# Routing five of eight batches inside the first attention instead of after it

## The reference, cut to what matters

```python
x = x + (o @ wo + bo)                         # end of the first attention (z in the kernel)
hn2 = layernorm(x, ln2_g, ln2_b).reshape(-1, 128)
logits = hn2 @ gate_w + gate_b                # 8 experts
idx = argmax(logits, axis=-1)                 # the first of equal ones
mid = relu(hn2 @ w1[e] + b1[e])               # 128 -> 512, for each expert e
y = mid @ w2[e] + b2[e]                       # 512 -> 128
moe = y[idx, token]                           # each token takes its own expert's row
```

## Time and profile before

| | us |
|---|---|
| median of three executions | 1964.28 |
| the profiled execution | 1971.45 |
| its span in the trace | 1969.7 |
| attention_l0, first reduce to last add | 339.5 to 711.1 |
| moe, first instruction to the first tile's transpose | 712.3 to 772.4 |
| moe, the loop over 40 tiles | 772.4 to about 885 |

### The profile page before, as it was taken

The page is one execution under the profiler, slowest core; times in us unless marked ns, Lnnn a source line. Parts: engine busy times, 40 slices in busy tenths (PEclk is TensorE's granted clock), DMA queues, the critical chain, the costliest instruction groups (busy, mean ns, idle before and its releaser), DMA issues. The chain is left out here.

```text
span 1969.7 us, 48105 instructions
## 1 busy us (share of the span) xinstructions
PE 1733.4 (88%) x18438; PEld 740.2 (38%) x18438; DVE 1569.2 (80%) x2889; ACT 1310.2 (67%) x2776; POOL 1120.2 (57%) x740
## 2 busy tenths in 40 slices
PE   6528856999999974986998999999999999999997
PEld 3327732233333353663442333333333333333334
DVE  7953467999999833547878999999999999999973
ACT  4502234789989932225884777888888878888885
POOL 8813542000100035331133988999999999989995
PEclk9869877799999975998997999999999999999998
DMA  2230036111111052117995323323223232232311
GB/s 49 33 55 3 1 100 241 40 50 40 49 40 50 23 177 71 50 48 256 367 405 164 88 73 81 86 68 88 73 81 87 66 88 75 78 83 70 87 29 43
DMA packets 194487, 180.14 MB, mean 91 GB/s; under 512 B 58740, under 2 KB 155124, under 8 KB 194052
## 3 DMA queue, kind: packets, MB, share of 16 engines
q1 hardware_dynamic: 185860, 170.01, 29.3%
q0 software_dynamic: 2944, 7.10, 1.1%
q10 hardware_dynamic: 5504, 0.73, 0.2%
HBM read 101.16 MB, written 75.26 MB: 90 GB/s over the span
## 5 line engine op out<-in xcount | busy, mean ns | idle before, releaser
L1038 ACT ACTIVATE probs_l<-exp_l 128x512 f32<-128x512 f32 x1024 | 575.6, 595 | 177.4 <-PE exp_l L1077 171.6
L976 DVE TENSOR_REDUCE maxima_l<-max_l 128x1 f32<-128x512 f32 x1024 | 640.1, 683 | 32.9 <-PE max_l L1122 32.9
L952 POOL TENSOR_TENSOR part_sums_l<-probs_l 128x1024 f32<-128x1024 f32 x256 | 604.1, 2360 | 91.7 <-ACT probs_l L1038 78.8
L1077 PE MATMUL exp_l<-q_stack_l,k_stack_l 100*128 100x512 f16 x1024 | 392.0, 384 | 3.3 <-ACT probs_l L1038 2.9
L1122 PE MATMUL max_l<-k_stack_l,q_stack_l 96*128 96x512 f16 x1024 | 386.8, 388 | 4.6 <-DVE pv_bank_l L968 3.8
L1361 DVE TENSOR_REDUCE maxima_l<-max_l 128x1 f32<-128x512 f32 x512 | 317.0, 682 | 16.7 <-PE max_l L1465 16.5
L1415 ACT ACTIVATE probs_l<-exp_l 128x512 f32<-128x512 f32 x512 | 279.3, 600 | 42.5 <-PE exp_l L1478 37.1
L1093 PE MATMUL pv_bank_l<-probs_l,v_ring_l 128*32 128x512 f32 x2048 | 273.9, 607 | 0.5 <-ACT probs_l L1038 0.5
L1077 PEld LDWEIGHTS exp_l<-q_stack_l,k_stack_l 100*128 100x128 f16 x1024 | 98.4, 97 | 395.0 <-ACT probs_l L1038 363.8
L1297 POOL TENSOR_SCALAR rstd_l<-squares_l 128x4 f32<-128x4 f32 x7 | 1.6, 235 | 344.6 <-ACT junk_l L1400 344.6
L958 POOL TENSOR_TENSOR part_sums_l<-part_sums_l 128x512 f32<-128x512 f32 x128 | 163.1, 1274 | 10.0
(11 more groups left out here) (303 smaller groups left out, 2454.9 us busy)
## 6 DMA issues: line engine op xcount, KB each, us to landing
scratch_qk_l<-parts_g SPq DMA_DIRECT2D x128, 256.0 KB, 9.4
q_stack_l<-scratch_qk_l SPq DMA_DIRECT2D x192, 128.0 KB
k_stack_l<-scratch_qk_l SPq DMA_DIRECT2D x192, 128.0 KB
scratch_v_l<-v_g SPq DMA_DIRECT2D x16, 1024.0 KB
v_ring_l<-scratch_v_l SPq DMA_DIRECT2D x64, 256.0 KB, 3.3
scratch_stack_l<-parts_c SPq DMA_DIRECT2D x16, 384.0 KB, 3.5
q_stack_l<-scratch_stack_l SPq DMA_DIRECT2D x64, 96.0 KB, 2.2
k_stack_l<-scratch_stack_l SPq DMA_DIRECT2D x64, 96.0 KB, 2.3
```

The lines of the kernel that those rows point to most:

```text
L952: pool.tensor_tensor(part_sums[:, i, h, :, :], probs[:, i, h, 0:2, :], probs[:, i, h, 2:4, :], ALU.add).then_inc(pair_sum.sem, 1)
L976: dve.reduce_max(maxima[:, s % 2, at % NT, at // NT:at // NT + 1], max_bank(n, at)[:, :], AX).then_inc(max_taken.sem, 1)
L1038: act.activation(probs[:, i, at // NT, at % NT, :], exp_ps[at % 2][:, :], ACT.Exp, scale=a.scale).then_inc(prob_tile.sem, 1)
L1077: pe.matmul(exp_ps[at % 2][:, :], ks[0:SHIFT_ROW + HG, slot, h, k * P:(k + 1) * P], qs[0:SHIFT_ROW + HG, slot, h, :], start=True, stop=Tru ...
```

## The change

Batches 0 to 4 are routed wholly inside `attention_l0`, one turn each, in turns 3 to 7. Batch b is handled in turn b + 3:

- PE, s = 1, p = 7: four transposes of its normalised rows into `misc`; ScalarE, s = 2, first position: the affine step `hT` from `misc`.
- PE, s = 2, p = 7: four narrow matmuls for its logits, and the two rank matmuls of batch b - 1, both into `misc`; ScalarE, s = 3, first position: one copy of both to SBUF (`scores`).
- GpSimd adds the gate's bias, VectorE takes at s = 3, p = 6 the maximum and the equality with it (two instructions with a wait between them), GpSimd makes the rest of the choice with products of "none so far" (`choose`), and then, one batch behind, the places (`destine`) and the four scatters.
- GpSimd now also waits at the end of the stage for all its 20 scatters.

`moe` keeps only batches 5, 6 and 7: 12 scatters in place of 32.

```diff
-ROWS_BESIDE = B - 1
+ROWS_BESIDE, ROUTED_BESIDE = B - 1, 5
+L0_ROWST_STEP, L0_LOGITS_STEP, L0_BEST_AT = 1, 2, 6
...
+            def choose(b):
+                at = slice(b * NT, (b + 1) * NT)
+                pool.wait_ge(scores_sb.sem, scores_sb.made(b, 0))
+                pool.tensor_tensor(logits[:, :, :], scores[:, 0, :, :], r.gate_b[:, :].unsqueeze(1).broadcast_to([P, NT, E_]),
+                                   ALU.add).then_inc(logits_taken.sem, 1)
...
+                pool.wait_ge(is_best_ready.sem, is_best_ready.made(b, 0))
+                did(pool.tensor_tensor(none_so_far[:, 0, :, :], ones_e[:, :, :], is_best[:, :, :], ALU.subtract))
+                settle()
+                for n, step in enumerate((1, 2, 4)):
+                    old, new = none_so_far[:, n % 2, :, :], none_so_far[:, (n + 1) % 2, :, :]
+                    did(pool.tensor_copy(new[:, :, 0:step], old[:, :, 0:step]))
+                    did(pool.tensor_tensor(new[:, :, step:E_], old[:, :, step:E_], old[:, :, 0:E_ - step], ALU.mult))
+                    settle()
...
+            def destine(b):
...
+                for width in (4, 2, 1):
+                    did(pool.tensor_tensor(place[:, :, 0:width], place[:, :, 0:width], place[:, :, width:2 * width], ALU.add))
+                    settle()
+                did(pool.tensor_copy(r.dest[:, at], place[:, :, 0]))
...
+                for k in range(b * NT, (b + 1) * NT):
+                    pool.indirect_dma_start(out=sorted_rows[:, :], out_offset=bass.IndirectOffsetOnAxis(r.dest[:, k:k + 1], 0),
+                                            in_=r.rows[:, k, :], in_offset=None).then_inc(scattered, 16)
...
+                if 0 <= b - 1 < ROUTED_BESIDE:
+                    choose(b - 1)
+                if 0 <= b - 2 < ROUTED_BESIDE:
+                    destine(b - 2)
+            pool.wait_ge(rows_ready.sem, rows_ready.made(ROWS_BESIDE - 1, 0))
+            pool.wait_ge(scattered, 16 * ROUTED_BESIDE * NT)
...
+                    if p == L0_BEST_AT and s == L0_LOGITS_STEP + 1 and 0 <= turn - 3 < ROUTED_BESIDE:
+
+                        dve.wait_ge(logits_taken.sem, logits_taken.made(turn - 3, 0))
+                        dve.tensor_reduce(best[:, :], logits[:, :, :], AX, ALU.max).then_inc(best_ready.sem, 1)
+                        dve.wait_ge(best_ready.sem, best_ready.made(turn - 3, 0))
+                        dve.tensor_tensor(is_best[:, :, :], logits[:, :, :], bc(best[:, :], E_), ALU.is_equal).then_inc(is_best_ready.sem, 1)
...
+            def rows_transposed(turn, s):
...
+            def logits_and_ranks(turn, s):
...
-            for b in range(B):
+            for b in late:
                 scatter(b)
```

More of the change, by code:

```diff
@@ L1294, in _ @@
+            pool.wait_ge(gate_loaded, 16 * 4)
             for b in range(ROWS_BESIDE):
@@ L1385, in _, with router_beside @@
         def _(act):
+            def router_beside(turn, s):
+                b = turn - 3
+                if s == L0_ROWST_STEP + 1 and 0 <= b < ROUTED_BESIDE:
+                    act.wait_ge(gate_loaded, 16 * 4)
+                    act.wait_ge(rowsT_ps.sem, rowsT_ps.made(b, 0))
+                    if b >= 1:
+                        act.wait_ge(scores_ps.sem, scores_ps.made(b - 1, 0))
+                    act.activation(hT[:, :], misc[:, :], ACT.Identity, bias=g.router.col[:, 1:2], scale=g.router.col[:, 0:1]).then_inc(rowsT_sb.sem, 1)
+                if s == L0_LOGITS_STEP + 1 and 0 <= b <= ROUTED_BESIDE:
+                    act.wait_ge(scores_ps.sem, scores_ps.made(b, 0))
+                    if b >= 1:
+                        act.wait_ge(logits_taken.sem, logits_taken.made(b - 1, 0))
+                    if b >= 2:
+                        act.wait_ge(rank_taken.sem, rank_taken.made(b - 2, 0))
+                    first, end = (0 if b < ROUTED_BESIDE else 1), (2 if b >= 1 else 1)
+                    act.copy(scores[:, first:end, :, :], misc[:, first * NT * E_:end * NT * E_].rearrange("p (i k e) -> p i k e", i=end - first, k=NT)
+                             ).then_inc(scores_sb.sem, 1)
             def moments_beside(turn, s, at):
@@ L1448, in misc_read @@
                     pe.wait_ge(y_taken.sem, turn - 1)
+                if s == L0_ROWST_STEP + 1 and 0 <= turn - 3 < ROUTED_BESIDE:
+                    pe.wait_ge(rowsT_sb.sem, rowsT_sb.made(turn - 3, 0))
+                if s == L0_LOGITS_STEP + 1 and 0 <= turn - 3 <= ROUTED_BESIDE:
+                    pe.wait_ge(scores_sb.sem, scores_sb.made(turn - 3, 0))
+            def rows_transposed(turn, s):
+                b = turn - 3
+                pe.wait_ge(o_ready.sem, o_ready.made(turn * U + s - OUT_LAG, 0))
+                pe.wait_ge(rows_ready.sem, rows_ready.made(b, 0))
+                for j in range(NT):
+                    ins = pe.transpose(misc[:, j * P:(j + 1) * P], g.router.rows[:, b * NT + j, 0:D], g.ident[:, :])
+                ins.then_inc(rowsT_ps.sem, 1)
+            def logits_and_ranks(turn, s):
+                b, r = turn - 3, g.router
+                pe.wait_ge(o_ready.sem, o_ready.made(turn * U + s - OUT_LAG, 0))
+                if b < ROUTED_BESIDE:
+                    pe.wait_ge(gate_loaded, 16 * 4)
+                    pe.wait_ge(rowsT_sb.sem, rowsT_sb.made(b, 0))
+                    for j in range(NT):
+                        ins = pe.matmul(misc[:, j * E_:(j + 1) * E_], hT[:, j * P:(j + 1) * P], r.gate_w[:, :], start=True, stop=True)
+                if b >= 1:
+                    at = slice((b - 1) * NT, b * NT)
+                    ranks = misc[:, NT * E_:2 * NT * E_]
+                    pe.wait_ge(chosen.sem, chosen.made(b - 1, 0))
+                    pe.matmul(ranks, r.below[:, :], r.choice[:, at, :], start=True, stop=False)
+                    ins = pe.matmul(ranks, r.ones[:, :], r.before[:, at, :], start=False, stop=True)
+                ins.then_inc(scores_ps.sem, 1)
             def step(turn, s):
@@ L1805, in moe @@
         logits_bank, rank_bank = mid_bank, y_bank[1]
-        r, last_b = g.router, B - 1
+        r, last_b, first_b = g.router, B - 1, ROUTED_BESIDE
+        late = range(first_b, B)
         w1, w2 = sb("w1", [P, E_, F_]), sb("w2", [P, E_, FT, D])
@@ L1991, in tabulate @@
                 dve.sem_inc(table_ready, 1)
-            did(dve.memset(before[:, 0, :], 0.0))
             take_moments(last_b)
-            choose(0)
             normalise(last_b)
-            destine(0)
-            choose(1)
-            for b in range(2, B):
+            choose(first_b)
+            for b in late[1:]:
                 choose(b)
                 destine(b - 1)
-            destine(B - 1)
+            destine(last_b)
             tabulate()
@@ L2039, in _ @@
         def _(act):
-            for b in range(B):
-                act.wait_ge(zT_ps.sem, zT_ps.made(b, 0))
+            for b in late:
+                act.wait_ge(zT_ps.sem, zT_ps.made(b - first_b, 0))
                 act.activation(hT[:, b % 2, :], zT_bank[b % 2][:, :], ACT.Identity, bias=col[:, 1:2], scale=col[:, 0:1]).then_inc(hT_ready.sem, 1)
@@ L2090, in _ @@
                 rank(b)
-            pe.matmul(logits_bank[0][:, 0:E_], ones[:, :], before[:, T, :], start=True, stop=True).then_inc(counted, 1)
+            pe.matmul(logits_bank[last_b % 2 - 1][:, 0:E_], ones[:, :], before[:, T, :], start=True, stop=True).then_inc(counted, 1)
             pe.wait_ge(experts_in, 64)
```

88 lines of the change are left out of this document (63 added, 25 removed).

## The result

The change made the kernel slower. Median after 1971.31 us (1967.73 to 1974.07, 10 runs), before 1965.42 us on the same chip (1960.45 to 1969.48, 10 runs): ratio 1.003, 95% interval 1.0018 to 1.0042, or 5.9 us more. The changed kernel was timed against before twice more, on two chips: 1.0031 (1.0018 to 1.0044) and 1.0031 (1.0015 to 1.0047). Forecast were 1950.0 us and a range up to 1966. One execution of a kernel further down, before_light, took 6406 us and is left out of its ratio.

A forecast was written before the change was run, and what follows sets the result against it. VectorE was taken as next to full in the attention, nothing as full for long in the router. Attention + 5.85, its end + 4.8 and router - 25.0 gave -14.3 us: 1950.0 us median, with 1942 to 1966 holding about 8 in 10.

The forecast's parts named there:

- The router before: Router, stage's first instruction to first tile's transpose: read as 60.0 us, to become 35, a gain of 25.0 us.
- Transposes and hT: Attention, PE's four transposes and ScalarE's copy after them: 0.40 us a batch, between 0.24 and 0.65.
- VectorE's two narrow instructions: Attention, s = 3, p = 6: 0.19 us each, 0.4 us a batch on the engine setting the pace; GpSimd not late.
- Logits and ranks: Attention, PE at s = 2, p = 7: 1.7 us of work mostly covered by VectorE's full banks; 0.35 us a batch.
- The last ranks and the partly filled turn: Attention's end: 0.1 us added for the last ranks, on top of 5.75 us for five batches.
- Bounds of the attention: Attention's extra for all five batches: between 3.2 and 13.8 us, from 0.64 to 2.75 a batch.
- Rival 1: The attention does not absorb the insertions: 2.75 us a batch, 8 us more, 1958 us; 13 in 100.
- Stage end: End of attention: GpSimd's last places, four scatters and 1.9 us landing make the next stage 4.8 us later, 3.5 to 6.
- Router after: Router with three batches: table at 19 to 21 us, first tile at 35, between 32 and 36.
- Rival 2: Router: a pause behind the weights hits the shorter chain; 1960 if late, 1970 to 1975 if early; 25 in 100.
- Rival 3: Router: something else, such as slowed tails, holds the first fetch; half the gain, 1962 us; 5 in 100.
- The marks listed as right or wrong: Profile signs: right if turns near 45.0 us, first tile near 758; wrong if turns above 46.5 or fetch past 36.

The follow-up runs named there:

- before_light: The kernel before with only expert 0's weights loaded, seven eighths of the weight transfers left out, every tile given to expert 0's; ratio 1.0004 to before.
- wide: The changed kernel with logits matmuls of 128 columns in place of 8, gate weights repeated 16 times; ratio 1.0038 to before.
- but_narrow: Changed kernel with four batches, one scatter a step and zeros out of the weights' way, but logits matmuls of 8 columns; ratio 0.9942 to before.
- all_four: Changed kernel with wide logits, four batches, one scatter a step and zeros out of the weights' way; ratio 0.9952 to before, 1957.7 us.
- but_zeros_behind: Changed kernel with wide logits, four batches and one scatter a step, but zeros behind the weights; ratio 0.9918 to before, 1957.4 us.
- but_five: Changed kernel with wide logits, one scatter a step and zeros out of the weights' way, but five batches beside the attention; ratio 0.9957 to before.
- spread: The changed kernel with one scatter a step of the attention instead of four in a row; ratio 1.0034 to before.
- routed4: The changed kernel with four batches routed in the attention instead of five; ratio 1.0043 to before.

## Why the prediction was wrong, step by step

Balance, from the marks of the profiles and with 52 for the first tile of before: attention +14.0, stage end +6.2, first tile 37.7 - 52 = -14.3, sum +5.9, where +5.9 was measured. Forecast were +5.85, +4.8 and -25.0. Of the 20.2 us missed, 8.2 lie in the attention and 1.4 in the stage end, which the profiles show; 2.7 in the router after, which they show too; and 8.0 in the router before, which is inferred.

- **The router before, 60.0 us.** The largest single term that failed, as far as the sums above can tell. The length was read rightly from the profile; that the timed runs have it too was assumed. The profiled execution was 7.2 us above the median, and I took those 7.2 us off the total as if they lay outside the parts that the change touches, when most of them may lie in the very part that it removes. 8.0 of the 20.2 us missed.
- **Transposes and hT**, 0.40 us a batch: measured 0.42. Right.
- **VectorE's two narrow instructions**, 0.4: the fourth-to-first step grew by 0.27. Right in mechanism, a little high.
- **Logits and ranks**, 0.35 us of 0 to 1.7: 0.92 us in the turns that keep the full clock (11.67 less 10.75), and 1.8 to 2.45 where the clock falls. The term that was mis-sized: I had the eight weight passes' length right (1.06 + 0.78 us), but VectorE's full banks cover less of it than assumed, and I left out that 8-column matmuls can lower the clock for what follows. In turn 3, which has no ranks yet, the wide kernel took 0.56 us more than before. Taking 0.56 for turn 3 and 0.92 for the others, the cover makes 2.5 us more than forecast and the clock 4.3 us (long turns 3, 4 and 6), 6.8 in all. This is the term that the experiments show directly, by wide and but_narrow.
- **The last ranks and the partly filled turn**, 0.1: turn 8 took 22.9 us instead of 20.6. Its second-to-third step was 8.51 us instead of 7.40, with the granted clock at 0.82 between 710 and 715. The kernel with one scatter a step has 7.39 there and a clock of 1.00, but all_four has 8.86 and before itself had 9.05 in its second profile; I can't say what sets it, nor that the change does. 2.3 us.
- **Bounds of the attention**, 3.2 to 13.8 us: 14.0, just outside. Rival 1 (the attention doesn't absorb the insertions, 13 in 100) came true in its size (8.2 us more); with its 1958 us the kernel would still have been faster, so it isn't the whole answer.
- **Stage end**, +4.8 (3.5 to 6): +6.2. The 1.49 us wait for the last ranks' copy was missed, and landing is about 3.3 us, not 1.9.
- **Router after**, 35 us (32 to 36): 37.7, 39.4 and 36.5 in three profiles. The order was right: first the table (19 to 21 forecast, 18.7 found), then what stands behind the weights. Rival 2, a pause in the shorter chain, didn't come in any profile; that its price of 1970 to 1975 holds the measured 1971.3 is chance. Rival 3, something else holding the first fetch, was true in small: the zeros, 3.6 us in the profile.
- The marks listed as right or wrong: turns 3 to 6 were 46.4, 47.0, 45.5 and 47.1 us by the steps, where 45.0 was named as right and above 46.5 as wrong; the stage change came at 731.0 where 723 was named, the first tile at 768.7 where 758 was, the first fetch 35.8 us into the stage, just short of the 36 named as wrong, and at 37.5 in the second profile. The last scatter of the attention began 5.6 us before the stage change, where 8 were named. 12 scatters in moe and no gap before the table were right.

## What to carry to other kernels

Before costing the removal of a stretch, ask whether the timed runs have it: where a stretch holds a pause that waits for nothing of the program, time a sibling kernel whose profile lacks it. That a profiled execution lies above the median is no proof of such a pause; here kernels without one lay up to 8.8 us above theirs. Work put into PE's list costs more than its own length where it lowers PE's clock: eight matmuls of 8 columns cost more than eight of 128. And a wait at a stage's end is paid in full by everything behind it; four batches routed beside the attention, with wide logits, beat both kernels (0.9952 with one scatter a step and 0.996 with four in a row, on two chips without the hole; 0.9918 with one a step on a chip with it, where four in a row had 0.9996; that chip's before is itself slower), where five with narrow logits lost.

## What the runs showed of the hardware that I had not expected

- Logits matmuls of 8 columns, 1.06 us for eight, were followed by 3 us of a granted clock of 0.50 in three turns of five, the same turns (3, 4 and 6) in four profiles of kernels with this attention, in other sets of three or four turns elsewhere; of 128 columns, never.
- Four row scatters issued 1.27 us apart stop PE, VectorE and ScalarE together for some 2 us in the groups of runs on two chips, until 2.1 to 2.3 us after the fourth is issued, and not in those on the others; the same program showed both. One scatter a step never did, neither on a chip that has the hole (but_zeros_behind, but_narrow and but_five, 11.42 us) nor elsewhere (spread, all_four). What stops the three engines was not found: no instruction's code was on its way in turn 6 of routed4's hole, and no engine waits for the scatters there.
- Seven eighths of the weight transfers less made before no faster in timed runs (1.0004), and the changed kernel 0.9% faster, some 17 us: 8.9 of them in its router, which they hold (37.7 against 28.8 us to the first tile), and 6.4 in the loop over tiles (112.9 against 106.5).
